# A selective scan with routed experts: the VectorE products of chunks 4 to 6 and the place of an early table

## The reference

```python
def _L0_attn_ref(x, W_B, W_C, W_dt1, W_dt2, b_dt2, log_A, D_skip):
    B_t = jnp.einsum('btd,nd->btn', x, W_B)
    C_t = jnp.einsum('btd,nd->btn', x, W_C)
    dt = jax.nn.softplus(jnp.einsum('btr,dr->btd', jnp.einsum('btd,rd->btr', x, W_dt1), W_dt2) + b_dt2)
    A = -jnp.exp(log_A)
    A_bar = jnp.exp(dt[..., None] * A[None, None])
    dB = (A_bar - 1.0) / (A[None, None] + 1e-08)
    B_bar = dB * x[..., None] * B_t[:, :, None, :]
    y = _selective_scan(A_bar, B_bar, C_t)      # h = a*h + b; y = sum over n of h*c
    return y + D_skip * x
...
    selected_expert = jnp.argmax(routing_weights, axis=-1)
    for e in range(num_experts):
        h = jax.nn.gelu(jnp.einsum('bsd,dh->bsh', x, W1[e]) + b1[e], approximate=False)
        y = jnp.einsum('bsh,hd->bsd', h, W2[e]) + b2[e]
        out = jnp.where((selected_expert == e)[..., None], y, out)
```

## Time and profile before

| | |
|---|---|
| median of three runs | 744.25 us |
| lowest, highest | 741.87, 744.76 us |
| the profiled execution's own time | 740.42 us |
| its span, first to last instruction | 738.7 us |
| busy: PE, DVE, ACT, POOL | 684.2, 545.9, 469.9, 471.4 us |

### The profile page before, as it was taken

One profiled execution on the slowest core, in us unless ns is written; L12 is line 12 of the kernel. 1 busy time (PEld: TensorE's weight loads), 2 busy tenths in 40 slices (PEclk: granted clock), 3 DMA queues, 4 the chain that ended last, 5 costly groups with the idle time before them and its releaser, 6 DMA issues.

```text
span 738.7 us, 17431 instructions
## 1 busy us (share of the span) xinstructions
PE 684.2 (93%) x5808; PEld 575.4 (78%) x5809; DVE 545.9 (74%) x968; ACT 469.9 (64%) x983; POOL 471.4 (64%) x595
## 2 busy tenths in 40 slices
PE   8799899999998997997997889989999999999997
PEld 7677677787777776776776779768899999987776
DVE  6889999989999989998999998776434333344442
ACT  3886998998998987887895595322323232323451
POOL 3799988988969887889998684033324343333331
PEclk9699999999999999999999999989999999999999
DMA  7867842343232423362453468311111111211010
GB/s 242 278 226 264 263 161 76 113 159 114 86 134 99 151 84 107 60 149 87 94 138 57 75 214 280 120 58 44 51 56 51 54 54 47 64 31 38 25 45 14
DMA packets 43216, 82.46 MB, mean 112 GB/s; under 512 B 5368, under 2 KB 13565, under 8 KB 43136
## 3 DMA queue, kind: packets, MB, share of 16 engines
q1 hardware_dynamic: 38016, 68.84, 30.6%
q0 software_dynamic: 5120, 12.60, 5.6%
HBM read 69.49 MB, written 13.51 MB: 112 GB/s over the span
## 4 chain that ended last, share of the span: by engine, by line
PE 61%; ACT 12%; POOL 11%; issue 10%; DVE 3%; DMA 1%; DVEq 1%; POOLq 0%; ACTq 0%; SPq 0%
PE WW L1182 15%; PE misc L1219 14%; PE WW L1059 11%; PE YY L1097 7%; POOL w_sb L667 7%; ACT w_sb L843 5%; ACT Csb L833 4%; POOL b_sb L648 2%; PE misc L1214 2%; PE WW L1176 2%; PE misc L977 2%; PE YY L1145 1%; DVE w_sb L1330 1%; PE misc L989 1%; ACT xin L813 1%
## 5 line engine op out<-in xcount | busy, mean ns | idle before, releaser
L667 POOL TENSOR_TENSOR w_sb<-w_sb,Csb 128x512 f32<-128x512 f32 x202 | 254.8, 1272 | 53.1 <-DVE w_sb L1330 47.6
L1059 PE MATMUL WW<-b_sb,xin 64*128 64x130 f32 (+2 forms) x2304 | 202.3, 292 | 28.5 <-DVE w_sb L1330 13.9
L1059 PEld LDWEIGHTS WW<-b_sb,xin 64*128 64x128 f32 x2304 | 167.9, 191 | 75.5 <-issue 36.9
L1330 DVE TENSOR_TENSOR_SCAN w_sb<-WW,hlast,w_sb 128x512 f32<-128x512 f32 x152 | 187.6, 1269 | 7.3 <-PE WW L1059 3.6
L843 ACT ACTIVATE w_sb<-dt,negA 128x512 f32<-128x512 f32 x256 | 169.8, 709 | 8.8 <-DVE w_sb L1330 5.8
L924 ACT ACTIVATE dt<-WW,b1c 128x128 f32<-128x128 f32 x256 | 72.8, 387 | 142.2 <-PE WW L1182 134.6
L1097 PE MATMUL YY<-sm,w_sb 128*128 128x128 f32 x1024 | 143.0, 285 | 7.4 <-DVE row L1387 7.4
L740 POOL DMA_INDIRECT y_out<-CbX,ocol x36 | 42.1, 1168 | 159.7 <-DVE CbX L1756 155.0
L1097 PEld LDWEIGHTS YY<-sm,w_sb 128*128 128x128 f32 x1024 | 114.1, 144 | 22.1 <-POOL w_sb L667 6.4
L1219 PE MATMUL misc<-w_sb,dt 128*128 x512 | 118.6, 386 | 1.7 <-DVE row L1489 1.4
L1219 PEld LDWEIGHTS misc<-w_sb,dt 128*128 128x128 f32 x512 | 96.8, 194 | 15.0 <-issue 2.6
(11 more groups left out here) (312 smaller groups left out, 825.7 us busy)
## 6 DMA issues: line engine op xcount, KB each, us to landing
w_sb<-c_rows SPq DMA_DIRECT2D x86, 256.0 KB
CbX<-c_rows SPq DMA_DIRECT2D x42, 256.0 KB
w_sb<-w_in SPq DMA_DIRECT2D x20, 512.0 KB, 6.3
token_rows<-row SPq DMA_DIRECT2D x8, 1024.0 KB
w_sb<-w_in SPq DMA_DIRECT2D x24, 256.0 KB
xin<-x_in SPq DMA_DIRECT2D x8, 512.0 KB, 3.9
w_sb<-x_in SPq DMA_DIRECT2D x7, 512.0 KB, 8.1
b_sb<-b_in SPq DMA_DIRECT2D x1, 780.0 KB, 8.4
```

The costliest lines, as they stand in the source:

```text
L667: eng.tensor_tensor(hc[g % NHC], hb_of(g), Csb[i % NCS][:, :], ALU.mult).then_inc(s_hcp, 1)
L1059: return eng.matmul(to[:, a:a + width], x_rows[rows, k, h * P:(h + 1) * P], band[rows, k, at:at + width], start=start, stop=not start, ski ...
L1330: eng.tensor_tensor_scan(hb_of(g) if pooled(g) else w_of(g), w_of(g), A[g % NA], hlast[(q - 1) % 2][:, h * N + n:h * N + n + 1] if q % NC ...
```

## The change

Chunks 4, 5 and 6 have two units whose products VectorE makes, n = 5 and 12, instead of three; unit 8's two products and its keeping of the last column go to GpSimd, and its two copies of C to ScalarE. Chunks 0 to 3 and 7 stay. `first_table` no longer stands at j = 30 and 31 of chunk 6 but in the last chunk: its five steps at (j, gap) = (1, 0), (1, 1), (2, 0), (2, 1) and (3, 0), that is after the second scan of unit 0 and between the scans of unit 1.

```diff
--- before.py
+++ after.py
@@ -27,7 +27,7 @@
 KD = D // P
 KH = H // P
 ITEMS = N * KD
-VECTOR_UNITS = [(1, 6, 9, 12)] + [(5, 8, 12)] * 6 + [(1, 4, 8, 10, 15)]
+VECTOR_UNITS = [(1, 6, 9, 12)] + [(5, 8, 12)] * 3 + [(5, 12)] * 3 + [(1, 4, 8, 10, 15)]
 POOLED = [g // KD % N not in VECTOR_UNITS[g // ITEMS] for g in range(ITEMS * NQ)]
 POOL_BEFORE = [0, *accumulate(POOLED)]
 BATCHES = ((0, 4), (4, 7), (7, 8))
@@ -1567,10 +1567,8 @@
                         choose(0, 2 * j + gap - 60)
                     if q == BATCHES[0][1] + 1 and j == 2:
                         place_tokens(0, (gap,))
-                    if q == NQ - 2 and j > 29:
-                        first_table(2 * j + gap - 60)
-                        if (j, gap) == (31, 1):
-                            first_table(4)
+                    if last and 0 <= 2 * j + gap - 2 <= 4:
+                        first_table(2 * j + gap - 2)
                     if last and (j, gap) == (15, 0):
                         keep_ids()
                     if last and (j, gap) == (28, 1):
```

## The result

The changed kernel takes 745.87 us (median of 16 runs, 743.81 to 749.32); the kernel before, beside it on the same chip, 743.02 us (16 runs, 740.28 to 744.76). The ratio is 1.0045 [1.0029, 1.0060]: slower by about 3 us, within the 0.5% named in the prediction, beyond the interval of the ratio.

A forecast was written before the change was run, and what follows sets the result against it. Bounds: TensorE from n = 8 to 12, then VectorE; in chunk 6 GpSimd, through ScalarE. 0.1 + 0.75 + 2.2 - 0.18 = 2.87, taken as 2.8, on 744.25 gives 747.0 us; range 742.5 to 751.0.

The forecast's parts named there:

- Chunk 4 (+0.1): Chunk 4: GpSimd's idle time takes the pair; ScalarE's added copies make TensorE's xnr1 fill about 0.1 us late.
- Chunk 5 (+0.75): Chunk 5: GpSimd runs 0.85 us late with the pair, and through ScalarE scan 12 starts 0.75 us later.
- Chunk 6 (+2.2): Chunk 6: GpSimd's 2.60 us pair meets 0.37 us idle, so scan 12 starts 2.2 us later through ScalarE's copies.
- the clock rival: Chunk 6, n = 9 to 12: new TensorE waits lower its clock, one stretch costing 2.0 us, total 749.0; chance 0.20.
- The table (-3.82, +3.82, -0.18): VectorE saves 3.82 us ending chunk 6, pays 3.82 heading chunk 7, less 0.18 us of waiting before scan 3.
- Nobody waits: Head of chunk 7: the table is done before TensorE needs its semaphore, so the move makes no engine wait.
- The test of chunk 7's first scan: Sign of being right: chunk 7's first scan about 0.8 us earlier than 396.78, unit 3's about 2.8 us later.
- VectorE's time counts: Chunks 4 to 6: VectorE is the true bound, each pair gives back 1.37 us, total 740.1; chance 0.10.
- Absorbed: GpSimd's lateness is carried into chunk 7 and the table fills a wait there, total about 744.1 us; chance 0.20.
- All three on the path: Chunks 4 to 6: ScalarE's or GpSimd's lateness reaches VectorE at 2.60 us per pair, total 752.1; chance 0.07.

The follow-up runs named there:

- e1: Kernel before with only the three pairs moved to GpSimd, the table staying at the end of chunk 6: 744.15 us, ratio 1.0055.
- e2: Kernel before with only the table moved to the head of chunk 7, as in the change: 741.57 us, ratio 1.0022.
- e4: Kernel before with only the pairs of chunks 4 and 5 moved to GpSimd, the table staying: 741.13 us, ratio 1.0015.
- e7: e3 with four places for the copies of C instead of three: 737.98 us beside 739.7, ratio 0.9970 to the kernel before.
- e3: Kernel before with only chunk 6's pair of unit 8 moved to GpSimd, the table staying: 744.21 us, ratio 1.0054.
- e11: The changed kernel with four places for the copies of C instead of three: 740.56 us beside 743.08, ratio 0.9956 to the kernel before.
- e10: Kernel before with only the table moved, its steps a little further forward than in e2: 742.3 us beside 743.08, ratio 0.9996.
- e12: The kernel before, unchanged, profiled once more in a single execution: 741.25 us.
- e9: The changed kernel measured and profiled once more, against the kernel before: 745.63 us beside 743.08, ratio 1.0033.
- e5: e2 with 24 unused identity transposes put into TensorE's wait: 743.14 us beside 739.7, ratio 1.0045 to the kernel before.

## Why the prediction was right, and where it was not

**The forecast.** 744.25 + 2.8 = 747.0 us, +0.38%; measured 745.87 us and +0.45% in the first comparison, +0.33% in the second. Direction and size hold. The size is in part luck. Measured by themselves, two terms are larger than forecast, the pair of chunk 6 by some 2 us and the table by another 2, and these errors have one sign; e1 and e2 together would be over 5 us. The measured 2.9 and 2.5 us agree with the forecast because the whole came out smaller than its parts, or because it was measured beside a slower kernel before; which, is open.

**Chunk 4 (+0.1).** Confirmed: 53.43 against 53.33, scan 12 at 37.02 against 36.92, and the same in e1 and e4. VectorE's pair, 1.37 us, brought nothing; it became waits for TensorE. Before scans 9, 10 and 12 VectorE waits 1.08, 0.66 and 1.29 us after the change, where it waited 0, 0.47 and 1.44.

**Chunk 5 (+0.75).** Confirmed, with about 0.8: scan 12 at 41.64, 41.38, 41.59 and 41.30 in the four traces with the pair, 40.43 to 40.83 in the seven without it that have the ring of three. From scan 5 to scan 12 alone it is 23.79 to 23.82 against 22.96 to 22.97. The rest of the chunk is 14.11 us in each.

**Chunk 6 (+2.2).** The path, from GpSimd over ScalarE's copies to the scan, is seen in the rows of ScalarE and GpSimd above, and the size is confirmed by e1, where scan 8 stands as before and scan 12 stands 2.21 us later. e7 shows that it isn't the ring of three that makes the pair cost: with four places it costs 1.0040. As a price in the medians the term is too small: e3 costs 0.54% [0.37, 0.71], 4.0 us. e3's trace shows one way to the rest, as the clock rival had it: a wait of TensorE before xnr1, the lower level, and 4.47 us instead of 2.2. The prediction had that wait at 1.5 us and the stretch at 2.0; 1.79 and 2.3 were seen. The forecast should have carried part of it. That isn't all: the four executions of e3 at a mean clock of 0.977 or more lie 3.2 to 4.1 us above the median before, and the difference from 2.2 is not explained.

**The table (-3.82, +3.82, -0.18).** Direct part right, conclusion wrong. It left VectorE's bound end of chunk 6 with 3.94 us and came back with 3.49; scan 3 of chunk 7 is 3.49 us later in its chunk. The step that failed is "Nobody waits". I had asked which semaphore the table raises and who waits for that one, and had not asked who waits for what stands behind the table on VectorE's queue. That was TensorE, for unit 1's products: it already waited 2.80 us at this head before the change, and 3.71 us in one piece with it. Behind scan 3 chunk 7 took 2.3 us (e2) to 2.7 (after) more in these traces, though not in e11's. e2's ratio has the table at +0.2%, and e10's at nothing, with the same steps two to four gaps further forward, on another chip. A smaller slip: the 12 us of idle time of GpSimd that the prediction puts behind unit 3 are those of the whole chunk; behind scan 3 it is 10.3 of 42.3 us.

**The test of chunk 7's first scan** failed: 0.8 us earlier was forecast; against the start of chunk 4 it came 0.7 later (168.03 us behind it instead of 167.35), as chunk 6 ran 1.3 us later to scan 12 than the sum had it. That excess is there at scan 5 already (19.65 against 17.83), ahead of the pair, behind the 10.24 us at the lower level; e10, with no pair moved, has it too (20.17). The scan of unit 3, forecast 2.8 us later, came 4.2 later on the same count.

**The rivals.** "VectorE's time counts" fell: every kernel with less of VectorE in chunks 4 to 6 is slower or the same. "Absorbed" fell as a result, but has a kernel of truth: in the two traces of the change the pair adds nothing from scan 8 to scan 12 (14.03 and 14.05 us, against 14.08 in e10). "All three on the path" fell with e4. The clock rival holds in part: in e3 for chunk 6, and in the change and in e2 at a place where I hadn't looked, the head of chunk 7.

## What to carry to other kernels

Before work is moved onto an engine's queue, list what stands behind it there and who waits for that, and not just who waits for its own result; TensorE, made to wait 3.71 us in one piece, also ran at its lower level for 6.83 to 17.07 us there, in four traces. An engine with a high share of busy time can be expensive to load (1.0054) and yet bring nothing measurable when relieved (1.0004), if the next one is close behind it. When a wait travels from one engine to another through a ring of buffers, try the size of the ring: one place more was worth 0.7% here, more than any placement of the pairs. And compare two variants only beside the same executions of the kernel before: here its own median was 739.26, 739.7, 743.02 and 743.08 us, a difference larger than the effect.

## What the runs showed of the hardware

The stretches at TensorE's lower level lie at the same places in separate executions of a kernel, to within the shift of the start (before and e12, after and e9), and last 3.41, 6.83, 10.24, 13.65 or 17.07 us. With the wait of 3.71 us came 13.65 us (e2), 17.07 us (after, e9) and 6.83 us (e11). The kernel before has a wait of 2.80 us at the same head, and 3.41 us at the lower level (e12, TensorE):

```profile
400.23 1.61 PE L1059 MATMUL WW<-b_sb,xin 64*128 64x130 f32 x18 [2.80 <-DVE w_sb L1330]
```

But a wait of 2.52 us in e1 was followed by none and one of 1.79 in e3 by 6.83, so the length of a wait alone does not foretell it. Feeding TensorE with 24 transposes in the wait did not hold the level (e5). The Trainium skill, page TensorE: Matmul & The Clock Gate, section What's actually happening, says that activity releases the throttle; e5 shows no benefit from activity of this kind, with its fall at 404.0, though that is 3.9 us after the last transpose and so doesn't speak against the sentence either.

What stays open: what decides which of the clock's patterns an execution falls into. The mean granted clock, which every execution has, tells some of them apart. The clearest case is e11: 737.1 to 737.7 us at 0.976 and above, 740.4 to 743.4 at 0.970 and below. Of 29 executions of the kernel before on the chip of e9 to e12, those at 0.972 and below take 742.4 to 745.5 us, those above it 739.7 to 743.3. But of 35 on the chip of e1 to e4, 26 lay between 737.4 and 740.4 us and 9 between 741.3 and 743.2, at mean clocks of 0.975 to 0.981 and 0.974 to 0.979, and there the clock alone doesn't tell the two groups apart.
